# Scan stage: two silus of the shared expert run as a pair, x1 one step later, and a copy in the routing replaced by a memset

## What is computed

```
x = x + scan(layernorm(x))     # selective state-space scan, 16 states per channel
x = x + ffn(layernorm(x))      # mixture of experts, 64 experts, 6 per token, plus a shared expert
x = x + attn(layernorm(x))     # causal attention, 16 heads over 4 key heads
x = x + ffn(layernorm(x))      # the same experts again
```

## Time and profile before

| | |
|---|---|
| median of three runs | 3323.77 us |
| the profiled execution, its own time | 3315.88 us |
| its span | 3314.1 us |
| busy TensorE, VectorE, GpSimd, ScalarE over the span | 86%, 54%, 47%, 39% |
| scan stage | 0 to about 1162 us, its tail to about 1240 us |
| first experts | about 1240 to 1750 us |
| attention | about 1750 to 2350 us |
| second feed-forward layer | from about 2350 us |

### The profile page before, as it was taken

The page is one execution under the profiler, slowest core; times in us unless marked ns, Lnnn a source line. Parts: engine busy times, 40 slices in busy tenths (PEclk is TensorE's granted clock), DMA queues, the critical chain, the costliest instruction groups (busy, mean ns, idle before and its releaser), DMA issues.

```text
span 3314.1 us, 38115 instructions
## 1 busy us (share of the span) xinstructions
PE 2852.6 (86%) x13772; PEld 1526.8 (46%) x13772; DVE 1783.8 (54%) x3707; ACT 1281.4 (39%) x2678; POOL 1541.4 (47%) x955
## 2 busy tenths in 40 slices
PE   4578878788888879888858999999799899999998
PEld 2454544455555544433324555555454443444443
DVE  5887987988798942221226665655323343222221
ACT  4555656465555611111106666667421120111110
POOL 5998888979788911112116555555300000222212
PEclk7678989889989979999988999999999999999999
DMA  4354453535344458999950000000144220899997
GB/s 169 134 176 141 152 178 117 184 114 190 130 165 160 141 202 303 350 347 343 342 163 1 26 27 26 26 14 14 64 148 147 92 73 21 282 355 328 342 351 192
DMA packets 198956, 557.66 MB, mean 168 GB/s; under 512 B 24944, under 2 KB 26864, under 8 KB 198256
## 3 DMA queue, kind: packets, MB, share of 16 engines
q1 hardware_dynamic: 181072, 514.19, 44.9%
q0 software_dynamic: 16640, 39.86, 5.3%
q10 hardware_dynamic: 1056, 1.18, 0.1%
HBM read 480.42 MB, written 74.74 MB: 168 GB/s over the span
## 4 chain that ended last, share of the span: by engine, by line
PE 52%; DVE 13%; POOL 10%; ACT 8%; DMA 7%; SPq 6%; issue 4%; POOLq 0%; DVEq 0%; ACTq 0%
PE bank L930 8%; PE bank L918 6%; PE bank L991 6%; PE bank L897 6%; POOL arena L1666 4%; PE bank L1038 4%; PE bank L1095 3%; DVE arena L1172 3%; SPq L1901 3%; SPq L1890 3%; PE bank L1072 3%; DMA out<-arena 3%; DVE bank L1172 3%; PE bank L1017 3%; POOL arena L1672 2%
## 5 line engine op out<-in xcount | busy, mean ns | idle before, releaser
L1666 POOL TENSOR_TENSOR arena<-arena 128x1024 f32<-128x1024 f32 x256 | 610.9, 2387 | 58.8 <-PE bank L869 47.5
L869 PE MATMUL bank<-arena 128*128 128x128 f32 x2048 | 314.8, 306 | 192.8 <-POOL arena L1672 192.6
L1525 ACT ACTIVATE bank<-arena 128x512 f32<-128x512 f32 x512 | 343.0, 688 | 317.3 <-DVE arena L1172 200.9
L1755 POOL TENSOR_TENSOR arena<-arena 128x2048 f32<-128x2048 f32 (+3 forms) x128 | 296.7, 2320 | 279.2 <-DVE arena L1393 279.2
L869 PEld LDWEIGHTS bank<-arena 128*128 128x128 f32 x2048 | 264.8, 158 | 281.0 <-POOL arena L1672 225.1
L930 PE MATMUL bank<-arena 128*128 128x512 f32 (+1 forms) x768 | 375.2, 634 | 15.8 <-DVE arena L1195 15.8
L1588 ACT ACTIVATE arena<-arena 128x256 f32<-128x256 f32 (+3 forms) x512 | 286.2, 562 | 196.9 <-DVE arena L1384 166.6
L1672 POOL TENSOR_TENSOR arena<-arena 128x512 f32<-128x512 f32 x256 | 325.8, 1273 | 75.9 <-DVE arena L1172 75.7
L1172 DVE TENSOR_TENSOR_SCAN arena<-bank,arena 128x512 f32<-128x512 f32 x256 | 310.8, 1214 | 73.0 <-ACT bank L1525 70.4
L991 PE MATMUL bank<-arena 128*64 128x352 f32 x2048 | 327.0, 473 | 0.0
L1172 DVE TENSOR_TENSOR_SCAN bank<-bank,arena 128x512 f32<-128x512 f32 x256 | 308.5, 1205 | 0.0
(11 more groups left out here) (136 smaller groups left out, 4199.7 us busy)
## 6 DMA issues: line engine op xcount, KB each, us to landing
arena<-scratch_bc SPq DMA_DIRECT2D x128, 1024.0 KB, 5.4
arena<-in_w_gate SPq DMA_DIRECT2D x128, 704.0 KB, 11.9
arena<-in_w_up SPq DMA_DIRECT2D x128, 704.0 KB, 14.7
arena<-in_w_down SPq DMA_DIRECT2D x128, 512.0 KB, 15.3
arena<-in_w_down SPq DMA_DIRECT2D x128, 192.0 KB, 17.7
scratch_x<-arena SPq DMA_DIRECT2D x16, 1024.0 KB, 4.3
scratch_xn<-arena SPq DMA_DIRECT2D x15, 1024.0 KB, 8.6
arena<-scratch_x SPq DMA_DIRECT2D x48, 256.0 KB, 5.7
```

What stands on the lines that cost most here:

```text
L869: i = nc.tensor.matmul(y[:, t * P:(t + 1) * P], w[:, n, t * P:(t + 1) * P], p.ident, is_transpose=True, start=False, stop=g == GROUPS - 1 ...
L1525: nc.scalar.activation(bank[p.da_bank(k, n)][:, :], block_of(p.dt, b, c), ACT.Exp, scale=p.alog[:, c, state:state + 1]).then_inc(*p.decaye ...
L1666: nc.gpsimd.tensor_tensor(out=p.hb[k % HB], in0=over(block_of(p.dtx, b, c), 1, NG), in1=p.bc[k // 2 % NBC][:, 0], op=ALU.mult).then_inc(*p ...
L1755: nc.gpsimd.tensor_tensor(out=own, in0=own, in1=over(p.rden[:, k % 2, :], 2, width), op=ALU.mult).then_inc(*p.divided.up(k))
```

## The change

1. `shared_units` takes two blocks j and j+1 at a time, in five pieces for six: gate j; gate j+1; both silus with up j; hid j with up j+1; hid j+1. The silus write two buffers `ssg`, so the silu of j waits for the hid of j-2, not j-1. The last pair makes its 64 wide gate and up together, ahead of the silus.
2. `x1`, and with it the front of the batch that it ends, comes in step k for the block whose last step is k-3, not k-2.
3. In the routing the copy of the six largest values into a tile `six` padded with -1 goes; the last two of the eight maxima are overwritten with -1 in place. The memset of `six` on GpSimd at the start goes too.
4. Memory: `list_memory` moves to another place, to make room for the second buffer.

```diff
 def shared_units(m, quads):
 
     for q in quads:
-        for j in range(SC):
-            last = j == SC - 1
-            yield [("sg", m, q, j)] + [("su", m, q, j)] * last
-            yield [("silu", m, q, j)] + [("fetch", m, q, 0) if last else ("su", m, q, j)]
-            yield [("hid", m, q, j)]
+        for j in range(0, SC, 2):
+            last = j + 2 == SC
+            yield [("sg", m, q, j)]
+            yield [("sg", m, q, j + 1)] + [("su", m, q, j + 1)] * last
+            yield [("silu", m, q, j), ("silu", m, q, j + 1), ("su", m, q, j)] + [("fetch", m, q, 0)] * last
+            yield [("hid", m, q, j)] + [("su", m, q, j + 1)] * (not last)
+            yield [("hid", m, q, j + 1)]
...
     def is_begun(piece):
-        return bool(piece) and piece[-1][0] not in ("hid", "so")
+        return bool(piece) and (piece[-1][0] not in ("hid", "so") or piece[-1][0] == "hid" and piece[-1][3] % 2 == 0)
...
-    for k in range(NSTEP + 2):
+    for k in range(NSTEP + 3):
...
-        if k >= 2:
-            b0, c0, g0 = step_of(k - 2)
+        if k >= 3:
+            b0, c0, g0 = step_of(k - 3)
...
-        f["ssg"] = sb.cut([BANK])
+        f["ssg"] = [sb.cut([BANK]) for _ in range(2)]
...
-        nc.vector.tensor_tensor(out=f["shT"][rows, j, :], in0=f["ssg"][rows, :],
+        nc.vector.tensor_tensor(out=f["shT"][rows, j, :], in0=f["ssg"][j % 2][rows, :],
...
-        nc.vector.tensor_copy(f["six"][:, :, 0:TOPK], f["top"][:, :, 0:TOPK]).then_inc(*p.routed.up(m, q, "six"))
+        nc.vector.memset(f["top"][:, :, TOPK:], -1.0).then_inc(*p.routed.up(m, q, "six"))
         V.wait_ge(p.routed, m, q, "six")
         for t in range(QT):
-            i = nc.vector.match_replace(out=marked[:, t, :], in_to_replace=f["six"][:, t, :],
+            i = nc.vector.match_replace(out=marked[:, t, :], in_to_replace=f["top"][:, t, :],
...
-        if (q, j) != (0, 0):
-            before = ("su", m, q, j - 1) if j else ("su", m, q - 1, SC - 1)
+        if (q, j) >= (0, 2):
+            before = ("su", m, q, j - 2) if j >= 2 else ("su", m, q - 1, SC - 2 + j)
             A.wait_ge(p.ring_with(*before).taken_by["dve"], *before)
-        nc.scalar.activation(f["ssg"][P - n:, :], bank[ring.bank("sg", m, q, j)][0:n, :],
+        nc.scalar.activation(f["ssg"][j % 2][P - n:, :], bank[ring.bank("sg", m, q, j)][0:n, :],
                              ACT.Silu).then_inc(*ring.taken_by["act"].up("sg", m, q, j))
...
-        nc.gpsimd.memset(f["six"], -1.0)
```

More of the change, by code:

```diff
@@ L523, in memory @@
         self.feed_forward(sb, 0)
-        self.list_memory(sb, 0)
         self.route_memory(sb, 0)
@@ L532, in memory @@
         self.gather_memory(sb, 0)
+        self.list_memory(sb, 0)
         assert sb.at <= behind
@@ L572, in list_memory @@
         f["wts"], f["key"], f["row"], f["gap"] = (sb.cut([NPAIR]) for _ in range(4))
-        f["own"], f["twice"] = sb.cut([1]), sb.cut([1])
+        f["twice"] = sb.cut([1])
         f["tok"] = sb.cut([CAP])
@@ L579, in route_memory @@
         f["mask"] = [sb.cut([QT, E]) for _ in range(2)]
+        f["own"] = sb.cut([1])
         f["less"], f["sum"], f["inv"] = (sb.cut([QT]) for _ in range(3))
-        f["top"], f["six"] = (sb.cut([QT, 8]) for _ in range(2))
+        f["top"] = sb.cut([QT, 8])
         f["rank"], f["code"] = (sb.cut([SEQ]) for _ in range(2))
```

## The result

| | before | after |
|---|---|---|
| median of the runs | 3325.8 us | 3346.6 us (6 runs, 3342.8 to 3356.7) |
| ratio to before, 95% interval | | 1.0073, 1.005 to 1.0096 |
| profiled execution, its span | 3315.9, 3314.1 us | 3356.4, 3354.3 us |
| last weighing of the scan stage | 1161.5 us | 1182.5 us |
| first expert matmul behind the tail | 1240.5 us | 1259.0 us |

The account below looks back on a forecast made before the run. GpSimd, VectorE and TensorE were all near full, GpSimd with the strictest chain, TensorE setting the pace at steps 14 to 23. Six batches +18.9, clock -2.6, seventh batch -1.5, tail -2.9: +11.9 on 3323.8, so 3336 us, range 3302 to 3352.

Parts of the forecast that it names:

- Blocks on TensorE: TensorE, steps 11 to 20: eight gate/up blocks for six, up block 1 waits for hid 0; +4.6, kept as +4.9 us.
- one kind at +4.1 and the other at +2.2: Net us per full batch: template batch +4.1; every second batch, which also has fold and picks, +2.2; three of each.
- The silu pairs on ScalarE: ScalarE: 47 fewer table loads against about 5 us of new waiting at Ln; 0 per batch, bounds -5.6 and +2.
- hid beside dt_sum: VectorE at the two dt_sum steps, where it is the bound: one hid more inside, +0.7 us per batch.
- x1 a step later: VectorE's wait for the sum before x1 goes, shortening GpSimd's wait behind the statistics: -1.5 us per batch.
- Six maxima: Routing on VectorE: without the copy the mask starts earlier but ends at the same time; 0, bounds 0 and -0.5 per batch.
- Seventh batch: The seventh batch of the scan stage was entered in the sum at -1.5 us.
- Tail: After the last scan, one down block and one shared output are gone from ahead of the fold: -2.9 us.
- A: Rival: table loads were the brake and up block 1 waits under 1 us; -20 us, 3304 us; chance 0.22.
- B: Rival, no change: the new wait exists but TensorE's clock holds at 1.00; 3323 us; chance 0.24.
- C: Rival, clearly slower: up block 4 also waits for silu 4 behind Ln, +18 us more, 3354 us; chance 0.13.
- D: Rival: a table switch holds ScalarE longer than its row, by another 1.28 us; 3298 us; chance 0.03.

Follow-up runs that it names:

- experiment 3: The changed kernel with one empty slot left behind every silu pair: 3298.3 us, ratio 0.9943 to before.
- experiment 7: The changed kernel with one empty slot behind the first silu pair only: 3308.2 us, ratio 0.9968 to before.
- experiment 4: The kernel before with the shared expert's silu replaced by a plain copy, without its table loads: 3293.6 us, ratio 0.9922 to before.
- experiment 5: The changed kernel with the shared expert's silu replaced by a plain copy, without its table loads: 3334.1 us, ratio 1.0053 to before.
- experiment 2: The kernel before with x1 and its front one step later and nothing else: 3327.9 us, ratio 1.0021 to before.
- experiment 8: The changed kernel with one empty slot behind the second silu pair only: 3328.9 us, ratio 1.002 to before.
- experiment 6: The changed kernel with an empty slot behind every silu pair, and x1 and the front back at their old step: 3305.2 us, ratio 0.9957 to before.
- experiment 1: The changed kernel with x1 and the front put back to their old step, pairs and memset kept: 3341.4 us, ratio 1.0079 to before.

## Why the prediction was right, and where not

The direction held, and the size was 21 to 24 us where 12 were forecast. The mechanism held in part only, and that the sum came near was partly luck. The term that gave the forecast its sign was TensorE's, at the dt blocks. Its eight blocks, its wait and its slow block are all there, but they are there in experiments 3 and 7 as well, and these are faster than before. What parts the changed kernel from these two is what the second and the last pair do to the decays and to TensorE behind step 15, and the prediction had put the silu pairs at 0. Point by point:

- **Blocks on TensorE.** Right in kind. Up block 0's wait of 3.11 us went (by its own rows it had cost 6.55 us with what hung on it, not 6.7); up block 1 waits 2.22 us for hid 0 (3.2 expected), and runs in 5.40 us behind it. In three of the six batches it does; in the other three the fold stands ahead of it and waits instead. In the template the batch became 3.7 us longer, +4.1 was expected. All six batches from 1 to 6 sum to +15.8 us (+4.6, +2.9, +5.0, -0.1, +3.7, -0.3), where the terms gave 18.9 - 2.6 = 16.3. The sum agrees, its parts less so: I had one kind at +4.1 and the other at +2.2, and their means are 4.4 and 0.8. Nor does it sit where I had it. Of the 15.8 us, steps 11 to 15 have 11.8, steps 16 to 19 have 12.3 and steps 24 to 31 have 6.4, while steps 0 to 10 give 11.5 back and 20 to 23 give 3.2.
- **The silu pairs on ScalarE, counted as 0.** This is the step that failed. The wait at step 24 came as computed, 5.38 us. Missed was the one of 8.35 us at step 19: I had followed the pair beside Ln and not the pair beside the `dtr` products, where the second silu waits for a gate behind a dense row of products. The exchange of 0 was two large terms: about -20 us for the loads that went and about +44 us for the places (experiments 4 and 5; TensorE's stretch and the memset are in the 44). My estimate per batch mixed the second with TensorE's term, so the sum came near by terms that made up for each other. That is luck.
- **hid beside dt_sum** (+0.7) was too small. Behind the second dt_sum, hid 5 is done at 891.1 and the first down block of the batch waits 9.44 us for it. Before, this wait was 1.4 us, once. What it costs is not its length, since TensorE has slack there; GpSimd's wait behind it is 1.06 us.
- **x1 a step later** (-1.5 a batch) was wrong in sign for the kernel before, +0.2% (experiment 2). The wait of VectorE for the sum did go, but in the template the first four steps last 17.8 us, as before, and in its place the product with the diagonal (L867) waits for x1 on TensorE, 8.2 us in five places, which I had put at some tenths of a us. The next block's first product uses the bank that x1 frees.
- **Six maxima** (0, bounds 0 and -0.5 a batch): alone it gains about 6 us, with 2 to 12 us in its interval. The two batches where the copy took 1.57 us gain far more than the bound, the last one loses 2.2 us.
- **Seventh batch** (-1.5): it grew by about 5, the largest single error of the sum. GpSimd waited in it four times, 4.3 us together; after, seven times, 9.5 us. The longest, 3.51 us instead of 1.96, is the weighing behind the routing with its scaling of 4.80 us. In every one of the twelve experiments this batch is longer than before too, by 2 to 11 us.
- **Tail** (-2.9): -2.5.
- **Rivals.** A needed up block 1 not to wait, and fell; but its condition was not what decides, since experiment 3 is faster with that wait. Its true part is that loads were a brake, worth 26 us in the kernel before. B needed the clock to hold behind the new wait, and it was 0.76; the ratio excludes it too. C named one more wait, at up block 4 for silu 4: it is there, 1.39 us at 875.25, and is a part of what is more than 12 us. D is not supported: removing some 97 loads gave 26 us, 0.27 us each, far below the 1.28 us of the row itself.

What stays open: how the 44 us divide between the waits. Moving the last pair is worth 9 us of the scan stage and the second 22 (experiments 8 and 7), or 18 and 17 by the ratios, but each moves everything behind it, and experiment 6 has the second pair at the step of the changed kernel without the loss. Open too is which wait loses the time in experiment 1, where none of the decays' is long.

## What to carry to other kernels

Batching activations by table saves loads, but it moves them: in a queue that runs in order the whole batch waits for its last input, and what is queued behind it waits too. Before packing such a pair, look on each engine for what stands behind it and on TensorE for what stands ahead of its last product; leaving one slot free behind each pair turned a loss of 0.7% into a gain of 0.6%, with the same work and six table loads more. Not any free slot does it: two slots beside the projections gained nothing. Turning the order round within a queue only moved the wait to who shares a bank with the batch, for more.

## What the runs showed of the hardware

- Beside GpSimd's long operations a 128x24 copy on VectorE took 0.48 to 1.57 us (0.18 alone), a 128x256 multiply 0.65 to 4.80 us (0.43 alone), a mask 0.39 to 1.88 us (0.29 alone). The held ones end 0.04, 0.28 and 0.15 us behind the end of a GpSimd operation. Which of them is held changes from batch to batch. The memset in the copy's place took 0.065 us in all eight batches, and MAX8 0.60 or 0.61 in all.
- A table load has 1.283 us in every row, before and after, whoever asks for it; what one is worth to the kernel ranged from 0.27 us (97 gone, before) to nothing that could be measured (50 gone, changed).
- Behind a wait of 2.22 us TensorE's granted clock was 0.76 over 7 us and a block took 5.40 us instead of 3.60. Behind 9.44 us of waiting a down block took 8.29 us in the template and 6.98 to 7.33 in three other batches, and the three down blocks after it 5.51 each.
